# A sorting stage whose counting products go from float32r to plain float32

## The reference, cut to what matters

```python
raw_scores = jnp.einsum('bsd,ed->bse', u, centroids)
s = jax.nn.softmax(raw_scores + expert_biases, axis=-1)
topk_vals, topk_idx = jax.lax.top_k(s, TOP_K)          # TOP_K = 2, 16 experts
g_topk = jnp.sum(jax.nn.one_hot(topk_idx, N_r, dtype=s.dtype) * topk_vals[..., None], axis=-2)
xe = jnp.einsum('bsd,eod->bseo', u, Wr) + br
routed = jnp.einsum('bse,bseo->bso', g_topk, xe)
```

## Time and profile before

| | us |
|---|---|
| median of three runs | 2928.01 |
| lowest and highest | 2927.31, 2934.45 |
| the profiled execution's own time | 2931.08 |
| its span in the trace | 2929.3 |
| PE busy in the span | 2753.8 |
| DVE busy in the span | 2100.4 |

### The profile page before, as it was taken

One profiled execution on the slowest core, in us unless ns is written; L12 is line 12 of the kernel. 1 busy time (PEld: TensorE's weight loads), 2 busy tenths in 40 slices (PEclk: granted clock), 3 DMA queues, 4 the chain that ended last, 5 costly groups with the idle time before them and its releaser, 6 DMA issues.

```text
span 2929.3 us, 46455 instructions
## 1 busy us (share of the span) xinstructions
PE 2753.8 (94%) x13570; PEld 2044.7 (70%) x13570; DVE 2100.4 (72%) x3550; ACT 1855.5 (63%) x2684; POOL 1972.4 (67%) x1177
## 2 busy tenths in 40 slices
PE   5888789687999999999999999999999999999997
PEld 4555489575667777777777777777777777777775
DVE  6888566696677777777777777777777777777774
ACT  4555322242777777777777777777777777777774
POOL 4667610673677777777777777777777777777775
PEclk9999999898999999999999999999999999999999
DMA  4442488795122222222222222222222223222222
GB/s 131 139 148 97 134 265 259 248 304 185 45 62 50 65 59 56 63 54 68 44 72 47 65 53 67 49 67 59 54 69 51 65 45 74 45 66 53 67 50 49
DMA packets 250638, 266.71 MB, mean 91 GB/s; under 512 B 95984, under 2 KB 196592, under 8 KB 250096
## 3 DMA queue, kind: packets, MB, share of 16 engines
q1 hardware_dynamic: 238192, 231.47, 29.9%
q0 software_dynamic: 12288, 33.57, 3.6%
HBM read 123.37 MB, written 73.92 MB: 67 GB/s over the span
## 4 chain that ended last, share of the span: by engine, by line
PE 72%; ACT 1%; POOL 1%; DVE 1%; issue 1%; DMA 0%; SPq 0%; POOLq 0%; ACTq 0%; DVEq 0%
PE psV_b L1640 8%; PE psV_b L1635 8%; PE psV_b L1636 8%; PE psS_b L1623 8%; PE psS_b L1622 8%; PE psN_b L1608 8%; PE psY_b L1568 4%; PE psX_b L1568 4%; PE psY_b L1569 4%; PE psY_b L1570 4%; PE psX_b L1569 4%; PE psX_b L1570 4%; POOL pp_lo_b L1378 1%; PE psN_b L1690 1%; DVE vals_lo_b L1540 0%
## 5 line engine op out<-in xcount | busy, mean ns | idle before, releaser
L1378 POOL TENSOR_TENSOR pp_lo_b<-pf_b,pp_hi_b 128x1024 fp32r<-128x1024 f32 x512 | 1236.3, 2415 | 578.6 <-ACT pp_hi_b L1413 491.8
L1499 DVE TENSOR_REDUCE negmax_b<-psN_b 128x2 fp32r<-128x1024 f32 x512 | 626.8, 1224 | 331.8 <-PE psN_b L1608 324.1
L1408 ACT ACTIVATE pf_b<-psS_b 128x1024 f32<-128x1024 f32 x512 | 525.6, 1027 | 225.5 <-PE psS_b L1623 222.3
L1622 PE MATMUL psS_b<-qA_b,kA_b 128*128 128x512 f32 x1024 | 405.6, 396 | 6.5 <-DVE qB_b L1523 5.2
L1623 PE MATMUL psS_b<-qB_b,kB_b 68*128 68x512 f32 x1024 | 406.4, 397 | 0.0
L1636 PE MATMUL psV_b<-pp_hi_b,vals_lo_b 128*64 128x512 f32 x1024 | 403.2, 394 | 0.0
L1635 PE MATMUL psV_b<-pp_hi_b,vals_hi_b 128*65 128x512 f32 x1024 | 401.8, 392 | 1.5 <-DVE vals_lo_b L1540 0.2
L1429 ACT ACTIVATE kA_b<-psX_b 64x512 fp32r<-64x512 f32 x256 | 151.9, 593 | 286.8 <-PE psX_b L1570 283.6
L1640 PE MATMUL psV_b<-pp_lo_b,vals_hi_b 128*65 128x512 f32 x1024 | 320.5, 394 | 5.0 <-POOL pp_lo_b L1378 5.0
L1608 PE MATMUL psN_b<-kA_b,qA_b 128*128 128x512 f32 x1024 | 322.3, 396 | 1.8 <-DVE negmax_b L1499 1.5
L1413 ACT ACTIVATE pp_hi_b<-pf_b 128x1024 fp32r<-128x1024 f32 x256 | 271.6, 1061 | 8.1
(11 more groups left out here) (209 smaller groups left out, 5641.6 us busy)
## 6 DMA issues: line engine op xcount, KB each, us to landing
kA_b<-kA_b SPq DMA_DIRECT2D x128, 256.0 KB, 3.0
qB_b<-qA_b SPq DMA_DIRECT2D x128, 256.0 KB, 2.9
inverse_b<-inverse_dram SPq DMA_DIRECT2D x256, 128.0 KB, 3.0
xs_e<-rows_dram SPq DMA_DIRECT2D x144, 128.0 KB, 3.6
results_dram<-ys_e SPq DMA_DIRECT2D x72, 256.0 KB, 3.8
x_a<-x_dram SPq DMA_DIRECT2D x16, 512.0 KB, 4.7
part_dram<-x_s SPq DMA_DIRECT2D x32, 256.0 KB, 2.1
acc_s<-part_dram SPq DMA_DIRECT2D x32, 256.0 KB, 4.7
```

Of the source, the lines that this page charges most:

```text
L1378: pool.tensor_tensor(pp[1][:, c], pf[:, c], pp[0][:, c].bitcast(F32), ALU.subtract).then_inc(pl_pool, 1)
L1408: a.activation(pf[:, c], psS[:], ACT.Exp).then_inc(exp_act, 1)
L1499: v.tensor_reduce(negmax[:, n.slot(2), 2 * c:2 * c + 2], psN[:], AX.X, ALU.max, negate=True).then_inc(mx_dve, 1)
L1622: pe.matmul(psS[:, t], kA[:, s, keys], qA[:, s], start=True, stop=False)
```

## The change

The three float32r tiles go. `before`, `behind` and `every` become the three slices of `masks`, in plain float32, and `mask` becomes plain float32 too. The three copies at L636 go with them. Both counting blocks issue the same products, on operands of the other kind.

```diff
@@ -185,9 +185,7 @@
         masks = sb("masks", [P, 3, P])
-        before = sb("before", [P, P], F32R)
-        behind = sb("behind", [P, P], F32R)
-        every = sb("every", [P, P], F32R)
+        before, behind, every = [masks[:, i] for i in range(3)]
@@ -218,7 +216,7 @@
-        mask = sb("mask", [P, 2, TB, NE], F32R)
+        mask = sb("mask", [P, 2, TB, NE])
@@ -630,11 +628,10 @@
                     v.wait_ge(const_pool, POOL_CONST)
-                    for to, of in ((before[:], masks[:, 0]), (behind[:], masks[:, 1]), (every[:], masks[:, 2]),
-                                   (kept.ident_r[:], kept.ident[:]), (rank_up[:], counts_i[:, 0:NE]),
+                    for to, of in ((kept.ident_r[:], kept.ident[:]), (rank_up[:], counts_i[:, 0:NE]),
                                    (ebase[:], counts_i[:, NE:2 * NE]), (jcol[:], counts_i[:, 2 * NE:2 * NE + 4])):
                         v.tensor_copy(to, of).then_inc(const_dve, 1)
-                    v.wait_ge(const_dve, 7)
+                    v.wait_ge(const_dve, 4)
@@ -668,9 +665,9 @@
                     picked = mask[:, q % 2].rearrange("p t e -> p (t e)")
-                    pe.matmul(psC[:, 0, 0:TB * NE], before[:], picked, start=(q == 0), stop=False, skip_group_check=True)
+                    pe.matmul(psC[:, 0, 0:TB * NE], before, picked, start=(q == 0), stop=False, skip_group_check=True)
                     for d in range(1, TB):
-                        mm = pe.matmul(psC[:, 0, d * NE:TB * NE], every[:], picked[:, 0:(TB - d) * NE], start=False,
+                        mm = pe.matmul(psC[:, 0, d * NE:TB * NE], every, picked[:, 0:(TB - d) * NE], start=False,
                                        stop=(d == TB - 1), skip_group_check=True)
@@ -707,9 +704,9 @@
-                    pe.matmul(psC[:, 0, 0:TB * NE], behind[:], picked, start=False, stop=False, skip_group_check=True)
+                    pe.matmul(psC[:, 0, 0:TB * NE], behind, picked, start=False, stop=False, skip_group_check=True)
                     for d in range(1, TB):
-                        mm = pe.matmul(psC[:, 0, 0:(TB - d) * NE], every[:], picked[:, d * NE:TB * NE], start=False,
+                        mm = pe.matmul(psC[:, 0, 0:(TB - d) * NE], every, picked[:, d * NE:TB * NE], start=False,
                                        stop=(d == TB - 1), skip_group_check=True)
```

## The result

The changed kernel takes 2940.72 us as a median against 2932.83 us for the kernel before in the same comparison (ten runs of each). The ratio is 1.0027 with a 95% interval of 1.0015 to 1.0039: 0.27% slower, or 7.9 us, where 8.5 us (0.29%) was forecast. One of the ten executions of the changed kernel took 6571.54 us, was left out of the ratio and was not traced; without it the median is 2940.22 us. The forecast's 2936.5 us was counted from a median of three runs, which lay 4.8 us lower than the median of ten; the measured 2940.7 is inside the range given. The profiled execution has a span of 2939.5 us.

The account below looks back on a forecast made before the run. Bound: a ring of waits between DVE, PE and ScalarE in `route`, not PE's busy share. First block 7.15 plus second 1.35, copies 0, makes 8.5 us on a median of 2928.0: 2936.5 us, range 2930 to 2943.

Parts of the forecast that it names:

- The price of an instruction: Counting blocks: each added instruction costs 0.112 us, set by its weight load; 0.45 us a block, range 0.14 to 0.47.
- rival D: Counting blocks: second instruction's load is hidden, only columns cost, 0.14 us a block; +2.5 us, 2930.5 us; chance 0.12.
- four passes with a load each: Counting blocks: each float32 pass an instruction with its own load; block grows 1.34 us, whole by some 25 us.
- The first block on the ring: Block ahead of transposes and L694: 0.45 us fully exposed in groups 1 to 14, 0.85 in group 0; sum 7.15 us.
- the ring: In `route`, DVE's mask, PE's block and products, ScalarE's squares, then DVE again wait in turn; period 19.78 us a group.
- The second block beside the ring: Block ahead of L727, L730 and next L659: hidden in groups 0 to 12, exposed in last three; 1.35 us.
- the slack of the tanh: ScalarE's tanh behind L659 starts 0.76 us after PE's burst ends, enough to hide the second block's 0.45 us.
- The copies: Three copies at the start, some 0.4 us of DVE, hidden by its wait for GpSimd; worth 0, 0.4 at most.
- The clock: Falls behind the first counting block, groups 6 and 8, 1.56 us each; sign of change unknown, two falls kept.
- rival B: Longer thin block brings clock falls in some three more groups, 4.7 us on top: +13.2 us, 2941.2 us; chance 0.19.
- A: Main case: first block exposed, second mostly hidden, two clock falls kept; +8.5 us, 2936.5 us; chance 0.50.

Follow-up runs that it names:

- the run with the second block alone: Kernel before with only the second counting block on plain float32, first block and three copies as before: 2998.14 us, ratio 1.0004 (0.9995 to 1.0014).
- the moved kernels: Kernel before with first counting block behind products L694: float32r 2913.97 us (0.9942), plain float32 2915.75 us (0.9942), bfloat16 2913.73 us (0.9947).

## Why the prediction was right, and where its terms were off

**The price of an instruction: right.** The added four cost 0.91 - 0.47 = 0.44 us a block for 0.45 forecast. Two instructions a call, each with a load, at 0.11 us. Neither rival D's 0.14 us a block nor the 1.34 us of four passes with a load each came. The length of a single load, which the prediction took off its bursts, is in this row of the kernel before:

```profile
220.54 0.19 PEld L671 LDWEIGHTS psC_a<-mask_a,before_a 128*128 128x128 f32 x1 [1.52 <-DVE mask_a L527]
```

**The first block on the ring: mechanism right, size a little high.** DVE's wait grew by 0.42 us (0.39 to 0.81) and, in the later groups, from 1.00 to 1.42. But up to group 9 the period grew by only 20.07 - 19.78 = 0.29 us. The prediction put all of the block's 0.45 us into the period, and this step was too high by a third in these groups. The other 0.13 us came back behind L599: in the kernel before, two operations that settle the places take longer in these groups than in the changed one, as a second trace of the kernel before shows against one of the changed kernel:

```profile
142.76 0.21 DVE L532 TENSOR_TENSOR spot_a<-psC_a,ebase_a 128x64 f32<-128x64 f32 x1
143.01 0.34 DVE L534 TENSOR_TENSOR one_a<-one_a,spot_a 128x128 f32<-128x128 f32 x1
143.39 0.29 DVE L535 TENSOR_REDUCE place_f<-one_a 128x8 f32<-128x128 f32 x1
143.71 0.26 DVE L536 CAST place<-place_f 128x8 uint32<-128x8 f32 x1
```

```profile
145.27 0.21 DVE L530 TENSOR_TENSOR spot_a<-psC_a,ebase_a 128x64 f32<-128x64 f32 x1
145.51 0.29 DVE L532 TENSOR_TENSOR one_a<-one_a,spot_a 128x128 f32<-128x128 f32 x1
145.84 0.29 DVE L533 TENSOR_REDUCE place_f<-one_a 128x8 f32<-128x128 f32 x1
146.16 0.17 DVE L534 CAST place<-place_f 128x8 uint32<-128x8 f32 x1
```

0.34 + 0.26 against 0.29 + 0.17 is 0.14 us. The long forms stand in groups 2 to 9 of all three traces of the kernel before, but for groups with a fall, and of the run with the second block alone; the kernels with a longer, shorter or moved first block have the short forms there. So it hangs on the phase of the engines to each other; what lengthens the operations was not tested. In the first group the distance to the next grew by 22.06 - 21.40 = 0.66 us on average over three traces each, for 0.85 forecast.

**The second block beside the ring: right but for a leak.** Where the prediction had it exposed, it was: the last two distances between masks grew by 19.48 - 18.62 = 0.86 us and, where the clock held, by 17.58 - 16.68 = 0.90, twice a block. Elsewhere a little comes through in groups 9 to 12; in the period it shows between groups 11 and 13, which grew by 19.55 - 19.01 = 0.54 us and not by 0.42. There the squares of the odd step now wait 0.65 us for PE, for 0.20 before, and DVE reaches L597 0.73 us behind L588, where it was 0.61 before (290.90 - 290.29) and is 0.73 with the second block alone (290.65 - 289.92):

```profile
294.62 0.39 ACT L417 ACTIVATE acc_s<-psR_a 128x256 f32<-128x256 f32 x1 [0.65 <-PE psR_a L691]
294.77 0.69 DVE L588 TENSOR_TENSOR x_s<-qw_a,qs_a 128x512 f32<-128x512 f32 x1
...
295.50 0.69 DVE L597 TENSOR_TENSOR qw_a<-psR_a,qw_bc_a 128x512 f32<-128x512 f32 x1
```

That is 0.12 us in each of four groups, 0.5 us. I had followed the slack of the tanh and of PE's next wait, but not that of the squares.

**The copies: right.** Nothing, by the run that puts them back.

**The clock: the term that was mis-sized.** I kept the falls as they were. Without any fall the counts of the ring give 0.66 + 5.1 + 1.3 = 7.1 us: 0.66 for the first group, 5.1 from group 1 to group 14 ((320.70 - 59.14) - 2 x 1.67 = 258.22 in the changed kernel, 312.04 - 58.92 = 253.12 in the trace of the kernel before that has no fall), 1.3 for the end of the stage from the mask of group 14 on (41.66 for 40.33 us where the clock held best). The stage itself grew by 366.2 - 354.8 = 11.4 us over three traces each. The first mask came 0.8 us earlier, so some 5 us of the growth are left for falls that the changed kernel has and the one before has not. Most of them come in the last two groups, at the end of the stage: it takes 44.76, 41.66 and 48.14 us in the three traces for 40.3 in each of the kernel before (granted clock 0.50 over 344 to 348 us in the first, 0.59 over 320 to 324 us in the third), which is 3.2 us more than the blocks account for. That is the price of rival B (4.7 us, chance 0.19), though not in the groups that it spoke of: within the stage B came nearer than A. The whole profiled span grew by only 8.9 us (2938.9 for 2929.9 as means of three); the remainder after the stage was 2.4 us shorter, within the spread of its own traces (2573.4 to 2578.2 before, 2569.8 to 2574.2 after). What made it shorter is open. So the agreement of 8.5 with 7.9 is partly chance: a ring term some 1.4 us too high, falls put at nothing that aren't, and a remainder whose difference three traces can't tell from none.

## What to carry to other kernels

When an engine's busy share is high but two engines wait for each other once a period, ask of each added instruction on which side of that wait it stands: the same 64 instructions cost 7.2 us on the ring and 1.2 us beside it, and moving the first block off it gained 17 us. For products as narrow as these count instructions with their loads of weights, not columns: here a format mattered by how many instructions a product became and by how fast its weights loaded. A block that only one late reader needs belongs behind the work that many wait for.

## What the runs showed that was not expected

- A load of 128 columns in bfloat16 follows the one before at 0.03 us; in float32r and in float32 at 0.11 us. Four products on zeros and ones took 0.11 us in place of 0.47.
- GpSimd's addition at L380 (128x4) takes 0.42 us beside the three copies of DVE, also where they are put back, and 0.23 us without them; what follows at DVE starts at 8.47 and 8.27 us. It leaves no mark on the first group.
- With the wait of 1.1 us ahead of a thin block taken out of TensorE's queue, no slow burst came between groups 1 and 14, in three kernels of three, with one trace each. The kernel in bfloat16 kept the wait and has none either, so which of the two matters, the wait or the length of the block, is open. In the last groups the clock falls in the moved kernels too (granted clock 0.50 over 320 to 324 us in float32r).
